# One input of VectorE's two-tensor instructions moved to PSUM in the gather passes of a four-layer graph network

## The reference

```python
h = relu(layernorm(x)); x = x + gcn(gcn(h, W1, b1), W2, b2)   # sums over edges of h[src] * dinv[src] * dinv[dst], self-loops
h = relu(layernorm(x)); x = x + capsules(h)                   # 8 capsules of 16; 3 rounds of
#   p = softmax(sum(z * u[dst]) over each capsule); u = l2norm(segment_sum(z * p, dst) + xc), z = xc[src]
h = relu(layernorm(x)); x = x + relu(mean(h[src], dst) @ W + b)   # nodes without an edge take h itself
h = relu(layernorm(x))
m = gelu(concat(h[src], edge_attr) @ W1 + b1) @ W2 + b2
x = x + layernorm(h + segment_sum(m, dst)) * gamma + beta
```

## Time and profile before

| | us |
|---|---|
| median of 3 runs (6459.97 to 6472.45) | 6468.09 |
| the profiled execution's own time | 6477.16 |
| its span, first to last instruction | 6475.4 |
| GpSimd busy | 4556.3 (70%) |
| VectorE busy | 3938.3 (61%) |
| TensorE busy | 3888.7 (60%) |
| ScalarE busy | 1749.6 (27%) |
| L620, 3920 indirect gathers, busy | 3924.6 |

### The profile page before, as it was taken

How to read it: one execution, slowest core, us unless ns; L and a number is a source line. 1 busy time by engine, 2 the same in 40 slices (tenths; PEclk the granted TensorE clock), 3 DMA queues, 4 the chain that set the end, 5 groups by cost and what they waited for, 6 DMA issues and landing times. The chain is left out here.

```text
span 6475.4 us, 124195 instructions
## 1 busy us (share of the span) xinstructions
PE 3888.7 (60%) x27584; PEld 3387.0 (52%) x27585; DVE 3938.3 (61%) x10115; ACT 1749.6 (27%) x3856; POOL 4556.3 (70%) x4723
## 2 busy tenths in 40 slices
PE   2555555555555476667668868845555554656565
PEld 1444444444445365555568868845455553444444
DVE  6333333455555577777788888874555555666666
ACT  1000000111111333333343343321111114444444
POOL 6777776777777677777646645637777776777775
PEclk9666666666666687877789989977877776878787
DMA  3222222222222355555567757732222221222221
GB/s 118 66 65 66 66 65 64 61 66 66 66 66 67 105 168 162 164 163 164 159 194 241 240 175 237 242 119 63 67 68 67 68 66 46 66 67 66 67 66 57
DMA packets 446427, 691.27 MB, mean 107 GB/s; under 512 B 89517, under 2 KB 204474, under 8 KB 446218
## 3 DMA queue, kind: packets, MB, share of 16 engines
q0 software_dynamic: 127936, 263.97, 15.8%
q10 hardware_dynamic: 210816, 255.92, 12.5%
q1 hardware_dynamic: 107594, 170.62, 7.8%
HBM read 504.02 MB, written 186.12 MB: 107 GB/s over the span
## 5 line engine op out<-in xcount | busy, mean ns | idle before, releaser
L620 POOL DMA_INDIRECT u_parts<-table,src x3136 | 3135.8, 1000 | 1096.3 <-issue 954.7
L691 PE MATMUL ps_sum<-msg,onehot 128*128 128x128 f32 x7808 | 1206.5, 303 | 167.1 <-DVE x L1184 64.2
L691 PEld LDWEIGHTS ps_sum<-msg,onehot 128*128 128x128 f32 x7808 | 1092.0, 213 | 356.1 <-issue 156.0
L1169 DVE SCALAR_TENSOR_TENSOR onehot<-dst,minus_row,iota 128x512 f32<-128x512 f32 x1220 | 914.8, 751 | 432.8 <-issue 274.6
L691 PE MATMUL ps_u<-u_parts,onehot 128*128 x2928 | 622.1, 382 | 817.5 <-SPq L484 745.2
L691 PEld LDWEIGHTS ps_u<-u_parts,onehot 128*128 128x128 f32 x2928 | 546.1, 280 | 884.7 <-issue 884.6
L620 POOL DMA_INDIRECT ring<-table,src x784 | 788.8, 1006 | 275.8 <-issue 238.4
L691 PE MATMUL ps_sum<-u_parts,onehot 128*128 x2928 | 582.2, 361 | 662.3 <-SPq L484 513.2
L691 PEld LDWEIGHTS ps_sum<-u_parts,onehot 128*128 128x128 f32 x2928 | 509.2, 262 | 743.8 <-issue 743.8
L792 ACT ACTIVATE wide_t<-ps_a 128x512 f32<-128x512 f32 x244 | 144.6, 593 | 2211.7 <-PE ps_a L653 2155.3
L1421 DVE TENSOR_TENSOR zu<-ps_u,ring 128x512 f32<-128x512 f32 x732 | 504.8, 690 | 349.5 <-PE ps_u L733 169.6
(11 more groups left out here) (168 smaller groups left out, 5558.0 us busy)
## 6 DMA issues: line engine op xcount, KB each, us to landing
ring<-z_rows SPq DMA_DIRECT2D x392, 256.0 KB, 3.3
hots<-hot_rows ACTq DMA_DIRECT2D x248, 256.0 KB, 3.2
hot_rows<-hots ACTq DMA_DIRECT2D x244, 256.0 KB
u_parts<-table,src POOLq DMA_INDIRECT x3136, 2.5
z_rows<-ring SPq DMA_DIRECT2D x196, 256.0 KB
table<-hots ACTq DMA_DIRECT2D x122, 256.0 KB
wide<-hot_rows ACTq DMA_DIRECT2D x120, 256.0 KB, 3.3
wide_t<-hot_rows ACTq DMA_DIRECT2D x120, 256.0 KB, 3.6
```

Of the source, the lines that this page charges most:

```text
L620: nc.gpsimd.indirect_dma_start(out=slot(p, c % slots)[:, t * P:(t + 1) * P], out_offset=None, in_=tables[p], in_offset=bass.IndirectOffset ...
L691: last = nc.tensor.matmul(sums[k % len(sums)][:, 0:P], lhsT=onehot[:, k % HOTS, t, :], rhs=rows(t), start=(t == 0), stop=(t == TILES - 1))
L1169: V.scalar_tensor_tensor(out=onehot[:, k % HOTS, :, :], in0=per_row(dst[:, ds(chunk * TILES, TILES)], [P, TILES, P]), scalar=minus_row0[:, ...
```

## The change

A PSUM bank is freed: `ps_c` becomes one bank and `ps_t` views `ps_a` and `ps_b`. The freed bank, `beside`, holds a copy of iota, of dinv, of rdeg, a column of ones, and two buffers of shares for CAPS1. VectorE's two-tensor instructions in the gather passes then read one tensor from PSUM. Biased products are written over the product in `ps_b`; capsule norms and the normalized rows of EDGE lie in `ps_c`. In MEAN the product with WE goes to `ps_b` as well, so it is issued a step later, at age 15, after the next window's product has been read; `multiply` waits for the rows before. In EDGE L1523, a one-tensor instruction, becomes a product of two.

```diff
-        ps_c = [psum(f"ps_c{i}", [P, TILES * P]) for i in range(2)]
-        ps_t = [bank[:, :].bitcast(bf16)[:, 0:TILES * P] for bank in ps_c]
+        ps_c = psum("ps_c", [P, TILES * P])
+        beside = psum("beside", [P, 512])
+        ps_t = [bank[:, :].bitcast(bf16)[:, 0:TILES * P] for bank in (ps_a, ps_b)]
+        iota_p = beside[:, 0:P]
+        dinv_p = beside[:, P:P + NB]
+        rdeg_p = beside[:, P + NB:P + 2 * NB]
+        one_p = beside[:, 2 * P:2 * P + 1]
+        share_p = [beside[:, 3 * P + i * TILES * CAPS:3 * P + (i + 1) * TILES * CAPS] for i in range(2)]
+        caps_p = ps_c[:, 0:GROUP * CAPS]
+        edge_h = ps_c[:, :].rearrange("p (t f) -> p t f", f=P)
...
             def multiply(s, m, age, weights):
+                if m == 2:
+                    pe.wait_ge(win_rows_ready, at + (STEPS - UNROLL))
...
             def multiply_rows(s, age):
                 pe.wait_ge(row_copied, at + UNROLL)
-                if not starts(s, age):
-                    pe.wait_ge(win_rows_ready, at + STEPS)
+                following = at + (STEPS * 2 + 2 * UNROLL)
+                pe.wait_ge(win_out, min(following, STEPS * 3) if at.fixed else following)
                 for t in range(GROUP):
-                    last = nc.tensor.matmul(ps_c[1][:, t * P:(t + 1) * P], lhsT=row_t[:, t, :],
+                    last = nc.tensor.matmul(ps_b[:, t * P:(t + 1) * P], lhsT=row_t[:, t, :],
...
-                    if p == MEAN and on(k, 14) and have(14):
-                        multiply_rows(s, 14)
+                    if p == MEAN and on(k, 15) and have(15):
+                        multiply_rows(s, 15)
...
             def biased(s, m, age, bias):
-                V.tensor_tensor(win_sum, product_of(s, m, age), per_feature(bias, GROUP), ALU.add)\
+                product = product_of(s, m, age)
+                V.tensor_tensor(product, product, per_feature(bias, GROUP), ALU.add)\
                  .then_inc(win_biased, UNROLL)
-                return win_sum
+                return product
...
                 V.scalar_tensor_tensor(out=onehot[:, k % HOTS, :, :],
                                        in0=per_row(dst[:, ds(chunk * TILES, TILES)], [P, TILES, P]),
                                        scalar=minus_row0[:, ds(row0, 1)],
-                                       in1=iota[:, 0:P].unsqueeze(1).to_broadcast([P, TILES, P]),
+                                       in1=iota_p.unsqueeze(1).to_broadcast([P, TILES, P]),
...
+            V.tensor_copy(dinv_p, dinv[:, :])
+            V.tensor_copy(rdeg_p, rdeg[:, :])
+            V.tensor_copy(one_p, ones[:, 0:1])
+            link(V.tensor_copy(iota_p, iota[:, 0:P]))
             dve.wait_ge(w_loaded, N_W)
             plain_pass(CONV1, conv1_window, 11)
...
-                        V.tensor_tensor(prob_n[:, two, :].rearrange("p (t c) -> p t c", c=CAPS),
+                        V.tensor_tensor(share_p[two].rearrange("p (t c) -> p t c", c=CAPS),
...
-                        message(V, two, chunk(2), two).then_inc(msg_ready, 1)
+                        message(V, two, chunk(2), share_p[two]).then_inc(msg_ready, 1)
...
-                                lambda into: V.tensor_scalar(into, acc[:, win, :], 1.0, None, ALU.mult))
+                                lambda into: V.tensor_tensor(
+                                    into, acc[:, win, :], one_p.unsqueeze(2).to_broadcast([P, GROUP, P]),
+                                    ALU.mult))
...
-                    V.tensor_tensor(win_sum, win_h, per_feature(GA, GROUP), ALU.mult)\
+                    V.tensor_tensor(edge_h, edge_h, per_feature(GA, GROUP), ALU.mult)\
                      .then_inc(win_biased, UNROLL)
...
-                    V.tensor_tensor(win_rows, win_sum, h[:, win, :], ALU.add).then_inc(win_rows_ready, UNROLL)
+                    V.tensor_tensor(win_rows, edge_h, h[:, win, :], ALU.add).then_inc(win_rows_ready, UNROLL)
```

More of the change, by code:

```diff
@@ L167, in build @@
         win_in = wide[:, 0, :, :]
-        win_sum = wide[:, 1, :, :]
         win_t = wide_t[:, 0, :, :]
@@ L602, in body @@
                     pool.wait_ge(share_ready, s + (G + 1))
-                    message(nc.gpsimd, k % 2, chunk(0), k % HOTS).then_inc(msg_ready, 1)
+                    message(nc.gpsimd, k % 2, chunk(0), prob_n[:, k % HOTS, :]).then_inc(msg_ready, 1)
                 over_steps(pool, ENGINE.Pool, body, 0, LONG)
@@ L671, in turn_rows @@
                 for t in range(GROUP):
-                    last = nc.tensor.transpose(ps_c[0][:, t * P:(t + 1) * P], win_h[:, t, :], ident[:, :])
+                    last = nc.tensor.transpose(ps_c[:, t * P:(t + 1) * P], win_h[:, t, :], ident[:, :])
                 last.then_inc(row_turned, UNROLL)
@@ L706, in body @@
                         turn_rows(s, 13)
-                    if p == MEAN and on(k, 14) and have(14):
-                        multiply_rows(s, 14)
-                over_steps(pe, ENGINE.PE, body, 14 if p == MEAN else 8, reach=0)
+                    if p == MEAN and on(k, 15) and have(15):
+                        multiply_rows(s, 15)
+                over_steps(pe, ENGINE.PE, body, 15 if p == MEAN else 8, reach=0)
             def caps_pass(n, p):
@@ L799, in copy_rows @@
                     act.wait_ge(row_mm, at + 0)
-                nc.scalar.activation(row_t.rearrange("p t f -> p (t f)"), ps_c[0][:, :], ACT.Copy)\
+                nc.scalar.activation(row_t.rearrange("p t f -> p (t f)"), ps_c[:, :], ACT.Copy)\
                   .then_inc(row_copied, UNROLL)
@@ L807, in root_window, with norm_window @@
                   .then_inc(win_root, UNROLL)
-            def norm_window(s, n, age, source, cols, func):
+            def norm_window(s, n, age, source, cols, func, into=win_h):
                 at = s.back(age)
@@ L813, in norm_window @@
                 for t in range(GROUP):
-                    last = nc.scalar.activation(win_h[:, t, :], source[:, t, :], func,
+                    last = nc.scalar.activation(into[:, t, :], source[:, t, :], func,
                                                 bias=shift_cols[:, cols, :][:, t, :],
@@ L1289, in conv1_window @@
                     read_window(s, 0, CONV1, 6,
-                                lambda into: V.tensor_tensor(into, acc[:, win, :], rows(dinv, win), ALU.mult))
+                                lambda into: V.tensor_tensor(into, acc[:, win, :], rows(dinv_p, win), ALU.mult))
                 if on(k, 11) and have(11):
@@ L1305, in conv2_window @@
                     read_window(s, 1, CONV2, 6,
-                                lambda into: V.tensor_tensor(into, h[:, win, :], rows(dinv, win), ALU.mult))
+                                lambda into: V.tensor_tensor(into, h[:, win, :], rows(dinv_p, win), ALU.mult))
                 if on(k, 11) and have(11):
@@ L1475, in mean_window @@
                     read_window(s, 2, MEAN, 6,
-                                lambda into: V.tensor_tensor(into, acc[:, win, :], rows(rdeg, win), ALU.mult))
+                                lambda into: V.tensor_tensor(into, acc[:, win, :], rows(rdeg_p, win), ALU.mult))
                 if on(k, 11) and have(11):
@@ L1489, in mean_window @@
                     dve.wait_ge(rows_stored, at.in_rounds(16, 16 * WINDOWS * 2))
-                    V.tensor_tensor(win_rows, ps_c[1][:, :].rearrange("p (t f) -> p t f", f=P),
+                    V.tensor_tensor(win_rows, ps_b[:, :].rearrange("p (t f) -> p t f", f=P),
                                     per_feature(BE, GROUP), ALU.add).then_inc(win_rows_ready, UNROLL)
```

10 lines of the change are left out of this document (5 added, 5 removed).

## The result

| | before | after |
|---|---|---|
| median, us | 6469.95 (4 runs, 6459.97 to 6472.45) | 6320.27 (4 runs, 6319.73 to 6322.43) |
| profiled execution, its span | 6477.16, 6475.4 | 6322.43, 6320.6 |
| GpSimd busy | 4556.3 | 4354.5 |
| VectorE busy | 3938.3 | 3919.5 |

The ratio is 0.9772 (95% interval 0.9755 to 0.9789): 2.3% faster, 150 us. The forecast was 6340.

A forecast was written before the change was run, and what follows sets the result against it. GpSimd's gathers were taken to bound CONV1, CONV2, CAPS1 and MEAN, and its own cycle EDGE. Gathers -142, EDGE +13 and MEAN's tail +1 make -128 us, from 6468.1 to 6340 us; 80% range 6312 to 6385.

The forecast's parts named there:

- Point 1: Onehots in the gather passes: iota in PSUM ends their stretching of gathers, 81.6 us in the four passes that count.
- Points 2 and 3: dinv, rdeg and biased products in PSUM save 36.4 us in CONV1, CONV2, MEAN; capsule norms and shares 28.8 in CAPS1.
- The 5 us withheld: Gather passes: 5 us left off the saving for short VectorE instructions on SBUF tiles and phases shifting against L1366.
- Point 4: EDGE: L1536, L1540 and L1523 stretch gathers by 22.8 us, which no one waits for, so no gain.
- Point 5: EDGE's cycle: dearer VectorE instructions, mainly L1523, add 0.22 us a window, +13 us over 57 windows; ends -3 and +33.
- Point 6: MEAN: the product with WE a step later costs nothing, with 3 us cover a window; +1 us allowed in the tail.
- Point 7: Before CONV1: four copies to PSUM, some 0.2 us each, hide under the first landing.
- A: PSUM is slower for VectorE to read, 65 ns more per instruction by the skill: 6358 or 6360 us; chance 0.12.
- B: MEAN becomes bound by its own loop and its 25 us are lost: 6365, at worst 6420 us; chance 0.12.
- C: L1169 still holds gathers through its pointer scalar and dst in SBUF; 81.6 us stay: 6421 us; chance 0.06.
- D: Gathers stay stretched because the lock is not of the second input, while EDGE gets dearer: 6482 us; chance 0.05.
- E: EDGE follows the gathers after all, another 45 us gained and no +13: 6282 us; chance 0.03.

The follow-up runs named there:

- e6: The kernel after with the onehots reading iota from SBUF again: 6410.55 us, ratio 0.9903 to the kernel before.
- e8: The kernel before with 16 one-element memsets on VectorE ahead of CONV1, shifting the EDGE loop's code: 6468.11 us, ratio 1.0005.
- e11: The kernel before with ScalarE's square root in EDGE issued a step later, at age 13 instead of 12: 6465.56 us, ratio 0.9996.
- e13: The kernel before with only MEAN's move, the product with WE to ps_b a step later: 6477.23 us, ratio 1.002.
- e7: The kernel after with EDGE's copy of the window's sums as a one-tensor instruction again: 6321.26 us, ratio 0.9772 to the kernel before.
- e12: The kernel after with two more 128-element VectorE instructions ahead of the window's copy in EDGE: 6321.89 us.

## Why the prediction was right, point by point

**What bounds.** Right: four passes followed the gathers one for one, EDGE did not.

**Point 1, iota: 81.6 us.** Right, 90 us measured by e6. **Points 2 and 3, the other tiles: 36.4 and 28.8.** Right in the sum, to 10 us: the four passes gave 151.7 us, less 90 for iota 62, against 65 (by e6's median against before, 56). The passes' own numbers came within 2.2 us each. The mechanism, a two-input instruction holding a gather at its index read only if both are in SBUF, was shown both ways, by the change and by e6. The first half of what the Trainium skill, "SBUF — State Buffer", section "Who interferes with whom", says fits; its inference that descriptor generation is not held by such an instruction must not be carried over to this indirect DMA, which has indices to read: 0.998 us against 0.944 in the mean. Whether the writing of descriptors is held too, no run shows.

**The 5 us withheld.** Wrong: L1382 holds 7.7 us, 1.2 more than L1366 did, and no short instruction took the place of the others. The other 5 us in the passes are more than covered by the free gather's 944 instead of 947 ns, 2.35 us a pass. That is not of the change: later runs of the kernel before with other edits (e8, e11, e13) show 944 as well.

**Point 4, EDGE's stretch: 0.** Right: 46 us of stretch went (63.5 to 17.4) and EDGE gave 3.0.

**Point 5, the cycle: +13 us. This step failed.** Its term was right (L1539 +0.26 us, L1554 at 740 rather than 688), its rule was not: I let the window grow with VectorE's chain. Had it done so, e7 would stand 15 us below the kernel after and e12 10 us above it; they stand 1.0 and 1.6 above. The earlier trace rows show the chain with TensorE's product and sum "at a low clock" on it, and I took their durations as fixed. The sum's is not: it goes from 1.89 to 1.61 us as it starts later against the clock. In place of +13 us EDGE gave -3.0, with the window at 17.07 as before. That the clock's rhythm is what holds it there is argued, as said above. The gap at the loop's branch, 0.22 us shorter in the kernel after, was not foreseen. It nearly cancels the copy's 0.26 there, so the kernel after alone would not have told the rule from the accident; e7, e8 and e12 do.

**Point 6, MEAN's move: 0.** Right in the kernel after; alone it costs 11.6 us, and by stretching, not by the wait that I priced. The cover stood: MEAN gave 27.9 us, and TensorE still waits for landings. **Point 7, copies.** Right: the first gather starts at 97.7 us, as before (97.8).

**Rivals.** A is out: L1545 678, L1539 687, the onehot 745 ns (755 before); no price for reading PSUM near the 65 ns of the Trainium skill, "VectorE: DVE Perf Modes", section on the TRN2 errata. B is out (MEAN -27.9), C by e6, D by the groups of gathers, and E by e7's windows and the 3.0 us.

**What would have shown it.** The signs for the gathers, L1539 and the slot waits came; MEAN's wait came at 4.7 us a window, just under its 5; that for EDGE's windows, 17.3 us, did not. The time of 6320 owes the gathers its size, and to some luck that it lies in the range: that reached to 6312 because point 5's lower end was -3 us, reached for another reason (cheaper instructions) than the one that came.

## What to carry to other kernels

If one engine's gathers are stretched by another's two-input reads, it pays to lay their starts over the other's instructions one by one: that gave the gain of each pass, to 2.2 us, before anything was built. Before pricing 0.2 us in a loop that repeats to 0.03 us, look whether TensorE's granted clock changes in the same rhythm; here steps of 0.18 to 0.26 us a window then gave nothing, and moving a table load away from TensorE's operand gave 30 us on one kernel. It gave nothing on the other, so test an edit on top of the change as well before calling it useless. And when time is added to a path on purpose, measure on the trace how much of it arrived: of 0.57 us of new instructions it was 0.18.

## What the runs showed of the hardware that was not expected

- A loop of four engines kept 17.07 us (two stretches of granted clock, 10.24 at full and 6.83 at half) over 0.44 us of difference in VectorE's path, and came back to it after six longer windows.
- The gap between a loop's branch and the first register load of its body was 0.465 us in EDGE of the kernel before and 0.249 with 16 instructions ahead of CONV1 and nothing else changed: where the code lies decides here.
- ScalarE's normalization takes 443 ns into PSUM and 478 into SBUF (128x128).
- One chip ran the same kernels 17.5% slower (7601 for 6468 us), with 1359 us of idling before TensorE's matmuls for which the profile shows no wait, where 3 to 10 us are usual. On it the change, 2.3% elsewhere, gave nothing. Why it is so was not found.
